# Two-layer cross-attention decoder on one core: a re-ordered third stage, FFN steps woven into the end of the first attention, contexts loaded at the stage boundary

## What is computed

```python
x = x + L0_xattn(layernorm(x), ctx, ctx)     # 16 heads of 8, causal mask, softmax, @ Wo
x = x + L0_ffn(layernorm(x))                 # ternary weights: rms-norm, 128->512, erf-gelu, rms-norm, 512->128
x = x + L1_xattn(layernorm(x), ctx, ctx)     # 16 heads of 64, relative positions, sigmoid gate, @ Wo, layernorm with gain and bias
x = x + L1_ffn(layernorm(x))                 # int8 quantized 128x128 product
# scores of L1: (hq + ub) . hk  +  shift( (hq + vb) . head_r ), divided by sqrt(128), mask, softmax over the 120 keys
```

## Time and profile before

| what | value |
|---|---|
| median of 3 runs | 462.59 us (461.73 to 464.74) |
| profiled execution | 462.21 us, span 460.4 us |
| mean granted TensorE clock | 0.967 of full speed |
| attn0 | about 5 to 131 us |
| ffn0 | about 124 to 175 us |
| layer1 | from 174.8 us to the end |

### The profile page before, as it was taken

How to read it: one execution, slowest core, us unless ns; L and a number is a source line. 1 busy time by engine, 2 the same in 40 slices (tenths; PEclk the granted TensorE clock), 3 DMA queues, 4 the chain that set the end, 5 groups by cost and what they waited for, 6 DMA issues and landing times.

```text
span 460.4 us, 16745 instructions
## 1 busy us (share of the span) xinstructions
PE 428.4 (93%) x6147; PEld 317.8 (69%) x6147; DVE 384.3 (83%) x1316; ACT 370.7 (81%) x1467; POOL 252.8 (55%) x370
## 2 busy tenths in 40 slices
PE   8999999988779989799999999999999999999781
PEld 7556556555547768577887887888788778787570
DVE  5899999998468985489888989989898998988974
ACT  1999999989724564379899899899889989989961
POOL 4488888878935651023244444553654555355684
PEclk9999999999669999899999999999999999999987
DMA  7150000000000002777566565766746766476100
GB/s 216 51 192 22 14 12 6 10 7 8 1 2 1 0 2 69 190 193 186 127 160 150 126 165 123 161 147 140 180 108 159 155 144 163 120 180 148 29 7 23
DMA packets 54392, 44.88 MB, mean 97 GB/s; under 512 B 43952, under 2 KB 49328, under 8 KB 54320
## 3 DMA queue, kind: packets, MB, share of 16 engines
q1 hardware_dynamic: 53616, 43.59, 38.6%
q10 hardware_dynamic: 704, 0.32, 0.2%
HBM read 22.92 MB, written 20.97 MB: 95 GB/s over the span
## 4 chain that ended last, share of the span: by engine, by line
PE 78%; DVE 11%; ACT 4%; POOL 3%; DMA 1%; issue 1%; SPq 1%; POOLq 0%
PE PS L964 68%; PE PS L1161 4%; PE PS L980 2%; PE PS L1141 2%; POOL prob L307 1%; ACT prob L488 1%; DMA ctx<-in_ctxT 1%; DVE relw L709 1%; DVE nmax L666 1%; DVE nmax L668 1%; DVE relr L714 1%; PE PS L1086 1%; DVE nmax L640 1%; DVE qT L699 1%; DVE probT L647 1%
## 5 line engine op out<-in xcount | busy, mean ns | idle before, releaser
L351 POOL TENSOR_TENSOR prob<-prob,rsum 128x480 f32<-128x480 f32 x64 | 62.6, 989 | 70.7 <-DVE rsum L832 37.4
L488 ACT ACTIVATE prob<-prob,nmax 128x120 f32<-128x120 f32 x256 | 100.3, 414 | 0.0
L417 ACT ACTIVATE prob<-PS,nmax 128x120 f32<-128x120 f32 x256 | 89.4, 394 | 3.3 <-DVE nmax L731 2.9
L307 POOL TENSOR_TENSOR prob<-prob,rsum 128x480 f32<-128x480 f32 x64 | 62.5, 986 | 22.1 <-DVE rsum L704 12.4
L417 ACT ACTIVATION_READ_ACCUMULATOR prob<-PS,nmax 128x1 f32 x256 | 61.7, 241 | 0.0
L488 ACT ACTIVATION_READ_ACCUMULATOR prob<-prob,nmax 128x1 f32 x256 | 56.3, 220 | 0.0
L964 PE MATMUL PS<-rT,qv 64*32 64x152 f32 x2048 | 48.1, 297 | 2.4 <-ACT relw L567 2.4
L964 PE MATMUL PS<-ctx,wk 128*128 128x120 f32 x288 | 43.9, 289 | 2.3 <-DMA ctx<-in_ctxT 2.3
L964 PEld LDWEIGHTS PS<-xnT,wq 128*128 128x128 f32 x288 | 36.8, 191 | 9.3 <-issue 6.8
L964 PEld LDWEIGHTS PS<-rT,qv 64*32 64x32 f32 x2048 | 28.6, 106 | 20.6 <-issue 18.6
L964 PE MATMUL PS<-xnT,wq 128*128 128x128 f32 x288 | 42.5, 285 | 0.0
(11 more groups left out here) (195 smaller groups left out, 1100.6 us busy)
## 6 DMA issues: line engine op xcount, KB each, us to landing
rel_scratch<-relw SPq DMA_DIRECT2D x128, 152.0 KB, 2.7
relr<-rel_scratch SPq DMA_DIRECT2D x64, 240.0 KB, 4.3
ctx<-in_ctxT SPq DMA_DIRECT2D x32, 60.0 KB, 1.9
out_x<-fin SPq DMA_DIRECT2D x16, 64.0 KB, 2.2
x_all<-in_x SPq DMA_DIRECT2D x1, 640.0 KB, 7.1
wr<-in_wr SPq DMA_DIRECT2D x1, 512.0 KB, 5.0
wq<-in_wq SPq DMA_DIRECT2D x1, 512.0 KB, 3.7
wk<-in_wk SPq DMA_DIRECT2D x1, 512.0 KB, 4.5
```

Source lines behind the costliest of these rows:

```text
L307: return pool.tensor_tensor(pr, pr, cols(rsum[p], g, HG).unsqueeze(2).to_broadcast([S, HG, SK]), ALU.mult)
L351: return pool.tensor_tensor(pr, pr, cols(rsum[p], g, HG).unsqueeze(2).to_broadcast([S, HG, SK]), ALU.mult)
L417: last = act.activation(cols(prob[p], n, SK), cols(scores, q, SK), ACT.Exp, bias=nmax[p][:, n:n + 1], accum_out=ssum[p][:, n:n + 1])
L488: last = act.activation(cols(pr, n, SK), cols(pr, n, SK), ACT.Exp, bias=bias[:, n:n + 1], accum_out=total[:, n:n + 1])
```

## The change

1. Order of layer1. Every engine's program for a step is put in another order, with other PSUM banks. On PE a step now reads:
   C content second half [s-2]; A transpose of the int8 operand [s-7], queries first half [s], output first half [s-4]; E groups 3 and 2 [s-4]; A keys second half [s-1], gate product [s-1], values second half [s-2], queries second half [s], int8 product [s-7], output second half [s-4], transpose of xn [s+1], keys first half [s-1], values first half [s-2]; B pairs 2, 3, 0, 1 [s]; C transposes [s-3], content first half [s-1]; B pairs 4 to 7 [s]; E groups 0 and 1 [s-3]; C transposes [s-3].
   The int8 block is one step later than before, so layer1 has 24 steps (0..23) and not 23. The copy of the second half of the keys goes from DVE to ACT, one step later. xn is computed for s+2 and not for s+1. On SP the output store (now of s-8) stands ahead of the context load.
2. crossing. attn0(14..18) and ffn0(-3..2) are woven together in an order of each engine's own; attn0(19) is gone. The gelu table load moves to the end of attn0(16) on ACT. The quantized weight's transposes move from attn0(17) to attn0(15), and POOL's last step on wdn from attn0(15) to attn0(17).
3. Contexts. The contexts and masks of layer1's elements 0 and 1 are loaded in ffn0(-3), once attn0's products are through; those of later elements keep their place and wait.

The core of the diff (bank numbers and the rest of the re-ordering left out):

```diff
-            peeled(attn0, LOOPS[0][1], NB + 1)
-            for s in range(3):
-                peeled(ffn0, s - 3, s - 2)
-                peeled(attn0, NB + 1 + s, NB + 2 + s)
-            peeled(ffn0, 0, LOOPS[1][0])
+            peeled(attn0, LOOPS[0][1], NB - 2)
+            crossing()
+            peeled(ffn0, 3, LOOPS[1][0])
...
-            peeled(layer1, LOOPS[2][1], NB + 7)
+            peeled(layer1, LOOPS[2][1], NB + 8)
...
+            def load_context(t, p):
+                at, mask_at = held(sp, t * SK), held(sp, t * S * SK)
+                sp.dma_start(ctx_sb[p][:, :], ctxT[:, bass.ds(at, SK)]).then_inc(A1[f"ctx_loaded{p}"], 16)
...
+                t, p = s, par
+                if on(t):
+                    after(sp, A1["hv_ps"], 2 * t - 2)
+                    if not isinstance(t, int) or t >= 2:
+                        load_context(t, p)
...
             def ffn0(s, par):
-                pass
...
+                if at_step(s, -3):
+                    sp.wait_ge(A0["qkv_ps"], NB)
+                    for t in range(2):
+                        load_context(t, t)
```

POOL, ACT, DVE and PE each have a crossing; POOL's, ACT's and PE's are:

```diff
+            def crossing():
+                attn0(14, 0)
+                ffn0(-3, 1)
+                attn0(15, 1)
+                ffn0(-2, 0)
+                attn0(16, 0)
+                attn0(17, 1)
+                ffn0(-1, 1)
+                attn0(18, 0)
+                ffn0(0, 0)
+                ffn0(1, 1)
+                ffn0(2, 0)
...
+            def crossing():
+                attn0(14, 0)
+                attn0(15, 1)
+                attn0(16, 0)
+                ffn0(-3, 1)
+                ffn0(-2, 0)
+                ffn0(-1, 1)
+                attn0(17, 1)
+                ffn0(0, 0)
+                attn0(18, 0)
+                ffn0(1, 1)
+                ffn0(2, 0)
...
+            def crossing():
+                attn0(14, 0)
+                attn0(15, 1)
+                ffn0(-3, 1)
+                ffn0(-2, 0)
+                ffn0(-1, 1)
+                attn0(16, 0)
+                ffn0(0, 0)
+                attn0(17, 1)
+                ffn0(1, 1)
+                attn0(18, 0)
+                ffn0(2, 0)
```

DVE runs ffn0(-3), attn0(14), attn0(15), ffn0(-2), attn0(16), ffn0(-1), attn0(17), ffn0(0), attn0(18), ffn0(1), ffn0(2). The key copy on ACT, and the pair of relative scores on PE that now stand side by side:

```diff
+                t, p = s - 1, 1 - par
+                if on(t):
+                    after(act, A1["rsum"], 4 * t - 4)
+                    act.activation(ez[p][:, :], PS[:, 7, 0:H], ACT.Exp, scale=-1.0).then_inc(A1["ez"], 1)
+                    act.activation(cols(kT[p], 1, 4 * SK), PS[:, 5, 0:4 * SK], ACT.Copy).then_inc(A1["kT1"], 1)
...
-                    for m in (0, 1):
-                        for e, bank in ((0, 0), (1, 3)):
+                    for m in (2, 3):
+                        for e, bank in ((0, 3), (1, 4)):
...
+                    for m in (0, 1):
+                        for e, bank in ((0, 1), (1, 5)):
```

More of the change, by code:

```diff
@@ L89, in decoder_kernel, with run_steps @@
         scratch = [nc.dram_tensor(f"rel_scratch{i}", (S, H * WIN + BLK), fp32, kind="Internal").ap() for i in range(2)]
-        def run_steps(e, attn0, ffn0, layer1):
+        def run_steps(e, attn0, ffn0, layer1, crossing):
             def peeled(step, first, end):
@@ new lines, in layer1 @@
+                t, p = s - 1, 1 - par
+                if on(t):
+                    dve.wait_ge(A1["content"], 2 * t + 1)
+                    dve.wait_ge(A1[f"relr0{p}"], 2 * loads(t, p))
+                    dve.tensor_tensor(cols(prob[p], 0, HG * SK), PS[:, 3, 0:HG * SK], cols(relr[p], 0, HG * SK), ALU.add)\
+                       .then_inc(A1["added0"], 1)
+                    dve.tensor_tensor(cols(prob[p], 1, HG * SK), PS[:, 7, 0:HG * SK], cols(relr[p], 1, HG * SK), ALU.add)\
+                       .then_inc(A1["added1"], 1)
@@ L1173, in layer1 @@
                 if on(t):
+                    pe.wait_ge(A1[f"ctx_loaded{p}"], loads(t, p))
+                    freed(pe, (A1["probT3"], t - 2, t - 3), (A1["relw2"], t + 1, t))
+                    for m in range(4, 8):
+                        last = mm(PS[:, 5, (m % 4) * SK:(m % 4 + 1) * SK], cols(wk1_sb, m, 2 * DK), ctx_sb[p][:, :])
+                    last.then_inc(A1["hk_ps"], 1)
+                    freed(pe, (F1["qT"], t - 5, t - 6), (A1["added1"], t, t - 1))
                     if at_step(t, 0):
@@ L1323, in layer1 @@
[L1323 to L1334 removed]
+                    freed(pe, (A1["kT0"], free, t + 2), (A1["added3"], t + 2, t + 1), (A1["probT0"], t, t - 1))
@@ new lines, in layer1 @@
+                    pe.wait_ge(A1["scaled0"], ready)
+                    pe.wait_ge(A1["scaled1"], ready)
+                    probs_transpose(p, 0, (6, 0)).then_inc(A1["probT_ps"], 1)
+                t, p = s - 1, 1 - par
+                if on(t):
+                    pe.wait_ge(A1["kT0"], t + 1)
+                    freed(pe, (A1["relw1"], t + 2, t + 1), (A1["u"], t - 2, t - 3))
+                    freed(pe, (A1["hv0"], t, t - 1), (A1["ez"], t + 1, t))
+                    for m in range(0, 4):
+                        for e, bank in ((0, 3), (1, 7)):
+                            half_ = slice(e * DK, (e + 1) * DK)
+                            last = mm(PS[:, bank, (m % 4) * SK:(m % 4 + 1) * SK], cols(qu[p], m, S)[half_], cols(kT[p], m, SK)[half_])
+                    last.then_inc(A1["content"], 1)
```

718 lines of the change are left out of this document (331 added, 387 removed), and 10 rows, old and new, of the table A1.

## The result

| kernel | median | lowest to highest | ratio to before |
|---|---|---|---|
| before | 464.46 us | 461.36 to 466.89 (9 runs) | |
| after | 458.58 us | 453.57 to 460.03 (9 runs) | 0.9862, 95% interval 0.9829 to 0.9896 |

The change makes the kernel 1.4% faster. The forecast was 442.3 us, range 436 to 453: the sign was right, the size was not, and the time lies outside the range. The profiled execution after took 454.79 us with a span of 453.0.

The account below looks back on a forecast made before the run. The prediction took PE's work and seams to bound the third stage, and latency at half clock the stage boundaries. 462.2 - 7.0 (steps) - 7.0 (crossing) - 6.4 (opening) + 0.5 (closing) = 442.3 us, range 436 to 453.

Parts of the forecast that it names:

- Seams on PE: Layer1's steps: fewer changes of tile shape save PE 0.75 us a step; ten steps at 0.7 less give -7.0 us.
- Three masks a step at 0.26 more are 0.8: DVE then has 14.9, still under 15.6: Layer1's steps: DVE's masks beside POOL's scalings each take 0.26 us more, leaving DVE under the 15.6 us step.
- rival 1: Layer1's steps: ACT or DVE takes PE's place, steps stay 16.3 us, opening loses 2.1; 451.4 us, chance 0.18.
- Crossing, -7.0: First to second stage: first gelu 5.9 us earlier, the next four intervals save 1.1; together -7.0 us, bounds -4 and -9.
- the second stretch at half clock: Crossing: PE at the 1.2 GHz level from 133.2 to 140.0 us; claimed to go, while the first stretch stays.
- Opening, -6.4: Layer1's first steps: early contexts give 4.3 us, steps 2 to 4 save 0.7 each; together -6.4 us.
- the shifted scores of element 0: Opening: late next after the contexts; nothing on PE needs their sum until step 2; if PE waits, -3 us is left.
- Closing, +0.5: From ACT's step 18 to the end: the chain's links stay, two wait for a later step; +0.5 us (-1 to +3).
- Rival 3: Crossing gains little: PE idles to half clock twice again and element 15's chain is pushed back; 447 us, chance 0.12.
- Rival 4: Layer1's steps: second half of shifted scores, read behind the context load, reaches DVE late; slower, 467 us, chance 0.04.

Follow-up runs that it names:

- f_both: Kernel after plus the holds of both f_scale01 and f_scale23 on POOL's layer1 scalings; 449.05 us, ratio 0.9688.
- f_scale01: Kernel after, with POOL's first scaling of probabilities in layer1 held until DVE's mask of the second head group has ended; 453.29 us, ratio 0.9754.
- f_scale23: Kernel after, with POOL's scalings of head groups 3 and 2 held until DVE's third mask, normalisation and scale chain are done; 449.29 us, ratio 0.9675.
- m_contend: Separate measurement, computing no result: DVE's layer1 operation forms four in a row, alone, then beside POOL's scalings; masks took 1.4 us each in place of 0.59.
- p_cross: Kernel before with only the new crossing of the first two stages; layer1 and context loads as before; 459.27 us, ratio 0.9871.
- f_cross: Kernel after, in the crossing DVE's copy of transposed probabilities put ahead of FFN work and POOL's last wdn add one step later; 456.68 us, ratio 0.9833.
- p_ctx: Kernel before with only the contexts and masks of elements 0 and 1 loaded at the start of the second stage; 464.91 us, ratio 0.9987.
- p_layer: Kernel before with only the new order of layer1; crossing and context loads as before; 460.51 us, ratio 0.9909.
- f_all: Kernel after with the edits of f_both and f_cross together; 447.35 us, ratio 0.9640.
- f_warm: f_all plus constant products on PE in the closing steps, which keep it busy and change no result; 446.06 us, ratio 0.9599.

## Why the prediction missed

- **Seams on PE** (0.75 us a step): right. It shows where DVE lets it: 15.67 a step in f_both.
- **"Three masks a step at 0.26 more are 0.8: DVE then has 14.9, still under 15.6"**: this is the step that failed. The 0.26 came from one pair of overlapping rows, where the mask started with 0.39 us of POOL's add of the bias left. A mask that starts just behind a scaling has 0.89 left and pays 0.75. The trace before had that price too, in the norm of xn, 0.34 us long otherwise:

```profile
210.49 1.93 POOL L351 TENSOR_TENSOR prob<-prob,rsum 128x480 f32<-128x480 f32 x2 [3.97 <-DVE rsum L832]
...
210.59 0.97 DVE L853 TENSOR_SCALAR xn<-x_all,mv,rstd 128x128 f32<-128x128 f32 x1
```

The count was off as well: two of four masks were hit, but a norm and a four-column product too, 2.1 us a step. By the forecast's own sum that makes 14.1 + 2.1 = 16.2, over 15.6; measured over the ten steps DVE is busy 15.6 of 16.33 us a step (some other operations got shorter) and PE 15.7, so each waits for the other some of the time. That shows a second fault in the step: it took a DVE that is busy for less than 15.6 to cost nothing. In f_scale01 DVE is busy 15.4 a step and the step is still 16.09; in f_scale23 it is busy 14.7 and the step is 15.71. That the step after is as long as the one before is chance: the bounds are not the same. The argument against rival 1, "POOL's large scalings never stretched DVE's adds", was true and beside the point: the adds read PSUM, and m_contend shows that such forms don't contend.
- **Crossing, -7.0**: -6.2 in its stretch, of which 0.9 is layer1's own start (last gelu to first query copy: 6.3 us before, 5.5 after); the last gelu itself comes 5.3 earlier, and p_cross gives 5.0. The scalings and the late add on POOL, which I let cancel against DVE's work, cost up to 0.8 by f_cross. The first gelu came at 129.57, not near 128; the second stretch at half clock did go. The first, 10.1 us long, which the forecast kept, shrank to 3.4 us.
- **Opening, -6.4**: that the sum came out is luck. 4.3 of it were put on the contexts; p_ctx shows 0 for them, and p_layer the full 6.4 without them. The text named what stood behind ("the shifted scores of element 0") but held that nothing on PE needed their sum before step 2. PE needed the bank that the sum frees. In the new order that wait is not there. No run parts the 6.4 into seams and waits.
- **Closing, +0.5** (bounds -1 to +3): mis-sized, +4.8. The forecast looked at the chain from step 18 to the end. These are ACT's last copies of an attention output, before and after:

```profile
446.70 0.60 ACT L515 ACTIVATE oT_pairs<-PS 128x512 f32<-128x512 f32 x1 [0.94 <-PE PS L964]
...
439.46 0.60 ACT L568 ACTIVATE oT_pairs<-PS 128x512 f32<-128x512 f32 x1 [1.02 <-PE PS L1003]
```

Behind them 13.7 us are left before and 13.5 after: the end did not grow. The 5 us lie ahead of them, in the last element's way from its queries to its output, 43.5 us before and 48.5 after. f_both has 46.2 there, so the new order is longer in the closing even with the long stretches gone. By whole closings: 57.23 before, 59.66 in f_both, 61.45 in f_scale01, each with 3.4 us at the 1.2 GHz level in its first 50 us; 62.01 after, with 6.8. So some 2.4 go with the new order, most of the rest with the stretches, and some with the clock. That last share isn't measured by itself: f_all, without the long stretches, has 62.96 with 13.7 us at that level, and f_warm 59.22 with none. Why the new order is longer there stays open.
- **The rivals**: rival 1 came in the steps, with DVE in PE's place; its other half, that the opening loses its 2.1, did not. Rival 3 did not come either: one stretch at half clock is left in the crossing, not two, and it gave 6.2 of 7.0. That the profiled 454.79 lies near the 456 of both together is chance; the closing made up the sum. Rival 4 did not come: nothing waits for relr in every step. The median of 458.58 lies in what the text called the same (457.9 to 467.2, chance 0.06), though the ratio's interval lies below 1.

With the failed step replaced (steps 0 in place of -7.0, and the closing's +4.8) the forecast's own sum is 462.2 - 0 - 7.0 - 6.4 + 4.8 = 453.6, beside the profiled 454.79. The median of 458.58 lies 3.8 above that execution, that of the kernel before 2.3 above its own.

## What to carry over

Moving an operation in one engine's order changes what runs beside it on another. Before trusting a reordering, lay VectorE's operations that have two SBUF inputs, or that scale, round or copy f32 from SBUF to SBUF, against GpSimd's in time, and price each meeting at nearly the whole rest of the other instruction, not at a mean; then ask whether that engine's slack was just spent by the same change. Slack counted in busy time alone is not enough: here DVE at 15.4 of 15.6 us still made the step 16.1. A wait on the engine that has time can be worth more than the work it delays.

A wait in a profile that ends last hides the ones that end just before it: remove it alone once, or read who else was late, before its length goes into a sum.

## What was unexpected in the hardware

- The loss is lopsided in m_contend. Eight scalings alone took 7.59 us; beside four masks 9.24, beside four norms 7.69, beside four roundings 7.59. DVE lost 2.4, 2.0 and 2.4 us in them, POOL 1.65, 0.1 and 0.
- Size is no protection: a variance of 128x2 took 1.24 us in place of 0.22 beside a 128x512 add, and a rounding of 128x128, 0.16 us alone, took 0.97 beside scalings.
- From 410 to 420 us PE is busy 7.63 us in f_both's trace and 7.83 in f_all's. Yet up to 432 us it then spends some 3 us at the 1.2 GHz level in the one and some 13 in the other, and the closings differ by 3.3 us.
